# Gather indices held in SBUF for the whole run and edge features loaded two blocks at a time, in a graph layer on one core

## The reference

```
h     = relu(layernorm(x))                       # 12500 x 64
h0    = edge_attr @ W0 + b0
g     = gelu(gelu(h0) @ W1 + b1) @ W2 + b2
score = (h0 + g) @ W3 + b3                       # one row of 64 per edge
msg   = h[src] * score                           # a gathered row per edge
wV    = segment_sum(msg, dst) / max(count(dst), 1)
out   = x + wV @ Wo + bo
```

## Time and profile before

| | |
|---|---|
| device time, median of 3 runs | 4045.06 us (4044.77 to 4045.06) |
| span of the profiled execution | 4042.3 us |
| outside the span, against the median | 2.8 us |
| busy: PE, PEld, DVE, ACT, POOL | 81%, 53%, 27%, 14%, 75% |
| mean granted TensorE clock | 0.785 of full |
| data moved | 174.70 MB, 43 GB/s |

### The profile page before, as it was taken

The page is one execution under the profiler, slowest core; times in us unless marked ns, Lnnn a source line. Parts: engine busy times, 40 slices in busy tenths (PEclk is TensorE's granted clock), DMA queues, the critical chain, the costliest instruction groups (busy, mean ns, idle before and its releaser), DMA issues.

```text
span 4042.3 us, 34777 instructions
## 1 busy us (share of the span) xinstructions
PE 3264.8 (81%) x12308; PEld 2146.4 (53%) x12309; DVE 1084.3 (27%) x2563; ACT 585.2 (14%) x838; POOL 3045.3 (75%) x3228
## 2 busy tenths in 40 slices
PE   4988888888888878888888788888887788888879
PEld 2655555555555555555555555555555555555557
DVE  7322222222222222222222222222222222222234
ACT  4211111111111111111111111111111111111111
POOL 7777777777777777777777777777777777777776
PEclk8977777777777777777777777777777777777778
DMA  5211111111111111111111111111111111111112
GB/s 145 48 40 40 40 40 40 40 40 40 40 40 42 40 40 40 40 40 40 40 40 40 40 40 40 40 40 40 41 41 41 40 40 40 40 40 40 40 37 60
DMA packets 217372, 174.70 MB, mean 43 GB/s; under 512 B 112108, under 2 KB 163821, under 8 KB 216920
## 3 DMA queue, kind: packets, MB, share of 16 engines
q0 software_dynamic: 103136, 105.82, 12.1%
q1 hardware_dynamic: 113536, 64.91, 6.0%
q10 hardware_dynamic: 616, 3.20, 0.2%
HBM read 167.28 MB, written 6.40 MB: 43 GB/s over the span
## 4 chain that ended last, share of the span: by engine, by line
POOL 73%; issue 24%; PE 2%; DVE 0%; DMA 0%; POOLq 0%; ACT 0%; DVEq 0%
POOL rows L332 73%; PE ps_h1a L539 0%; PE ps_h1b L539 0%; PE ps_h0a L463 0%; POOLq L353 0%; PE ps_h1b L471 0%; PE ps_h1a L471 0%; PE ps_sb L482 0%; PE ps_sb L477 0%; PE ps_wa L497 0%; PE ps_h0b L463 0%; DMA rows<-h_rows,idx 0%; PE ps_sb L486 0%; PE ps_sa L482 0%; PE ps_sa L477 0%
## 5 line engine op out<-in xcount | busy, mean ns | idle before, releaser
L332 POOL DMA_INDIRECT rows<-h_rows,idx x3175 | 2999.5, 945 | 967.6 <-issue 966.9
L497 PE MATMUL ps_wa<-ln_sq,msg 128*128 128x128 f32 x1616 | 350.1, 385 | 665.6 <-DVE msg L690 665.5
L497 PEld LDWEIGHTS ps_wa<-ln_sq,msg 128*128 128x128 f32 x1616 | 299.2, 276 | 741.2 <-issue 728.1
L690 DVE TENSOR_TENSOR msg<-ps_sa,rows 128x512 f32<-128x512 f32 x202 | 139.7, 691 | 1403.3 <-DMA rows<-h_rows,idx 1391.0
L690 DVE TENSOR_TENSOR msg<-ps_sb,rows 128x512 f32<-128x512 f32 x201 | 139.0, 692 | 1396.8 <-DMA rows<-h_rows,idx 1382.0
L396 ACT ACTIVATE g<-ps_h1a,wp 128x512 f32<-128x512 f32 x202 | 139.0, 688 | 2383.5 <-PE ps_h1a L471 2383.5
L482 PE MATMUL ps_sa<-w_attr,attr 128*128 128x256 f32 x808 | 405.0, 654 | 0.0
L482 PEld LDWEIGHTS ps_sa<-w_attr,attr 128*128 128x128 f32 x808 | 229.8, 314 | 327.0 <-issue 292.6
L477 PE MATMUL ps_sa<-b_last,wp 1*128 1x512 f32 x404 | 403.1, 1097 | 0.0
L486 PEld LDWEIGHTS ps_sa<-w_gelu,g 128*128 128x128 f32 x1616 | 377.5, 321 | 34.3
L486 PE MATMUL ps_sa<-w_gelu,g 128*128 128x128 f32 x1616 | 367.7, 405 | 0.0
(11 more groups left out here) (94 smaller groups left out, 2381.4 us busy)
## 6 DMA issues: line engine op xcount, KB each, us to landing
attr<-in_edges SPq DMA_DIRECT2D x402, 128.0 KB, 3.0
rows<-h_rows,idx POOLq DMA_INDIRECT x3175, 2.4
xs<-in_x SPq DMA_DIRECT2D x4, 700.0 KB
h_rows<-ln_d ACTq DMA_DIRECT2D x4, 700.0 KB
dst_i<-in_dst SPq DMA_DIRECT2D x1, 1612.0 KB, 27.2
idx<-in_src SPq DMA_DIRECT2D x50, 32.0 KB, 2.3
rows<-in_dst_rows SPq DMA_DIRECT2D x4, 384.0 KB
out<-ln_d SPq DMA_DIRECT2D x1, 1530.0 KB
```

Of the source, the lines that this page charges most:

```text
L332: pool.indirect_dma_start(rows[:, slot, t, :], None, table, bass.IndirectOffsetOnAxis(ap=idx[:, part, at, t:t + 1], axis=0),).then_inc(gat ...
L497: pe.matmul(window[0:m * D, 0:m * WIN], msg[:, s % 2, t:t + m, :].rearrange("p t d -> p (t d)"), hot[:, k, t:t + m, :].rearrange("p t n -> ...
L690: dve.tensor_tensor(msg[:, s % 2, 0:n, :], ps_s[s % 2][:, 0:n * D].rearrange("p (t d) -> p t d", d=D), rows[:, s % G_RING, 0:n, :], ALU.mu ...
```

## The change

1. `idx` has room for all 403 blocks. The first 32 blocks' indices come as before, in four loads. The other 371 blocks' indices are loaded in 3 transfers with runs of 4 KB, a block on each partition, into `src_rows` (which lies in `ln_d`), after `raw_ready` reaches 3. DVE turns them into float32 (`number_src`, in its step 2). In PE's steps 4 to 9 (`turning_step`) `turn` transposes them by 4 matmuls a step with a unit matrix (`diag`), into the bank `ps_h0` of that step, and DVE copies them back as integers to `idx` (`keep_turned`, in its steps 3 to 8). PE waits for that copy ahead of `first(b + 2)`.
2. POOL builds a 128x128 ramp for `diag` at its start, and `gather` waits for indices 4 + 3 times in the run instead of 51 times. SP no longer waits for `msg_done` nor loads groups.
3. `load_attr` brings two blocks by one transfer, in runs of 2 KB, block by block: the even block on partitions 0 to 63, the odd one on 64 to 127. `first` becomes one matmul with 64 rows and 512 columns; the attribute part of `last` becomes 4 matmuls with 64 rows and 128 columns each. The amount of data is the same.

The diff, without the constants, the semaphores' declarations and the branch for wide windows that this input doesn't take:

```diff
@@ -234,27 +246,40 @@
         def tiles_of(b):
             return LAST_TILES if isinstance(b, int) and b == NB - 1 else TILES
+        src_rows = ln_d[:, :, :, :].rearrange("p k n d -> p k (n d)")[:, 0:TURN_CHUNKS, 0:BLOCK]
+        def chunk(c):
+            first = IDX_FIRST + c * P
+            return first, min(P, NB - first)
         block = ctx.enter_context(nc.Block())
         @block.sync
         def _(sp):
-            def load_idx(group, part, n=IDX_GROUP):
-                sp.dma_start(idx[:, part, 0:n, :],
-                             src[bass.ds(group * IDX_GROUP, n), :, :].rearrange("b p t -> p b t")
-                             ).then_inc(idx_in[part], 16)
+            def load_idx(q):
+                at = q * IDX_GROUP
+                sp.dma_start(idx[:, at:at + IDX_GROUP, :],
+                             src[at:at + IDX_GROUP, :, :].rearrange("b p t -> p b t")
+                             ).then_inc(idx_in[q], 16)
+            def load_src(c):
+                first, n = chunk(c)
+                sp.dma_start(src_rows[0:n, c, :].bitcast(I32),
+                             src[first:first + n, :, :].rearrange("b p t -> b (p t)")
+                             ).then_inc(src_in, 16)
             def load_attr(b):
                 n, half = min(2, NB - b), b // 2 % (IN_RING // 2)
-                halves = edges[b:b + n, :, :, :].rearrange("o g f (j c) -> j (g f) o c", j=2)
-                for j in range(2):
-                    sp.dma_start(attr[j * 2 * DE:(j + 1) * 2 * DE, half * 2:half * 2 + n, :, :
-                                      ].rearrange("p o k e -> p o (k e)"), halves[j]
-                                 ).then_inc(attr_in[half], 16)
-            load_idx(0, 0)
+                sp.dma_start(attr[0:n * 2 * DE, half, :],
+                             edges[b:b + n, :, :, :].rearrange("o g f c -> (o g f) c")
+                             ).then_inc(attr_in[half], 16)
+            load_idx(0)
             for c in range(LN_STEPS):
                 cols = slice(c * LN_ROWS, (c + 1) * LN_ROWS)
                 for p0, p1 in ((0, SPLIT), (SPLIT, NP)):
@@ -267,12 +292,12 @@
                                  ).then_inc(rows_in[c], 16)
             sp.dma_start(wp[:, :], weights).then_inc(weights_in, 16)
             load_attr(0)
-            load_idx(1, 1)
+            load_idx(1)
             sp.dma_start(dst_i[:, :, :], dst).then_inc(dst_in, 16)
             for b in range(2, IN_RING, 2):
                 load_attr(b)
-            for part in range(2, IDX_GROUPS):
-                load_idx(part, part)
+            for q in range(2, IDX_GROUPS):
+                load_idx(q)
             sp.dma_start(x_late[:, :, :], x[N_EARLY:N, :].rearrange("(t p) d -> p t d", p=NP)
                          ).then_inc(x_late_in, 16)
@@ -284,27 +309,13 @@
                          ).then_inc(base_in, 16)
             sp.dma_start(top[:, :], bounds_dram[1:2, 0:NB]).then_inc(base_in, 16)
-            def ahead(b, s):
-                if b % 2 == 1 and b + IN_RING - 1 < NB:
-                    sp.wait_ge(score_done, b + 1)
-                    load_attr(b + IN_RING - 1)
-            GROUPS = -(-NB // IDX_GROUP)
-            def group_ahead(group, part, n=IDX_GROUP):
-                for u in range(IDX_GROUP):
-                    ahead(group * IDX_GROUP + u, group * IDX_GROUP + u)
-                sp.wait_ge(msg_done, group * IDX_GROUP + IDX_GROUP)
-                load_idx(group + IDX_GROUPS, part, n)
-            for group in range(GROUPS - IDX_GROUPS):
-                group_ahead(group, group % IDX_GROUPS,
-                            min(IDX_GROUP, NB - (group + IDX_GROUPS) * IDX_GROUP))
-            for b in range((GROUPS - IDX_GROUPS) * IDX_GROUP, NB - IN_RING + 1):
-                ahead(b, b)
+            sp.wait_ge(raw_ready, len(jobs) - LN_STEPS)
+            for c in range(TURN_CHUNKS):
+                load_src(c)
+            for b in range(1, NB - IN_RING + 1, 2):
+                sp.wait_ge(score_done, b + 1)
+                load_attr(b + IN_RING - 1)
             for half in range(2):
                 k0, k1 = half * len(groups) // 2, (half + 1) * len(groups) // 2
@@ -322,16 +333,20 @@
         def _(pool):
             pool.iota(iota_i[:, :], pattern=[[1, WIN]], base=0, channel_multiplier=0
                       ).then_inc(set_up, 1)
+            pool.iota(diag_i[:, :], pattern=[[1, P]], base=0, channel_multiplier=-1
+                      ).then_inc(diag_set, 1)
             def gather(b, s, table):
-                slot, part, at = s % G_RING, s // IDX_GROUP % IDX_GROUPS, s % IDX_GROUP
-                if at == 0:
-                    pool.wait_ge(idx_in[part], uses(b, IDX_GROUP * IDX_GROUPS) * 16)
+                slot = s % G_RING
+                if s < IDX_FIRST and s % IDX_GROUP == 0:
+                    pool.wait_ge(idx_in[s // IDX_GROUP], 16)
+                if s >= IDX_FIRST and (s - IDX_FIRST) % P == 0:
+                    pool.wait_ge(idx_ready, ((s - IDX_FIRST) // P + 1) * (TILES // TURN_TILES))
                 for t in range(tiles_of(b)):
                     pool.indirect_dma_start(
                         rows[:, slot, t, :], None, table,
-                        bass.IndirectOffsetOnAxis(ap=idx[:, part, at, t:t + 1], axis=0),
+                        bass.IndirectOffsetOnAxis(ap=idx[:, s, t:t + 1], axis=0),
                     ).then_inc(gathered[slot], 16)
             for b in range(RAW):
@@ -458,12 +473,11 @@
             def first(b, s):
                 if s % 2 == 0:
-                    pe.wait_ge(attr_in[s // 2 % (IN_RING // 2)], uses(b, IN_RING) * 32)
-                for j in range(2):
-                    mm = pe.matmul(ps_h0[s % 2][:, j * 2 * P:(j + 1) * 2 * P], w_in[:, j, :],
-                                   attr[:, s % IN_RING, :, :].rearrange("p k e -> p (k e)"),
-                                   start=(j == 0), stop=(j == 1), skip_group_check=True)
-                mm.then_inc(h0_done, 1)
+                    pe.wait_ge(attr_in[s // 2 % (IN_RING // 2)], uses(b, IN_RING) * 16)
+                o = s % 2
+                pe.matmul(ps_h0[s % 2][:, :], w_in[o * 2 * DE:(o + 1) * 2 * DE, o, :],
+                          attr[o * 2 * DE:(o + 1) * 2 * DE, s // 2 % (IN_RING // 2), :], start=True, stop=True
+                          ).then_inc(h0_done, 1)
             def second(b, s):
@@ -477,10 +491,12 @@
                 pe.matmul(ps_s[s % 2][:, :], one_row.to_broadcast([1, P]),
                           b_last[0:1, :, :].rearrange("p t d -> p (t d)"), start=True, stop=False,
                           skip_group_check=True)
-                for k in range(2):
-                    four = ps_s[s % 2][:, :].rearrange("p (j k c) -> p k j c", j=2, k=2)[:, k, :, :]
-                    pe.matmul(four, attr[:, s % IN_RING, k, :],
-                              w_attr[:, :].rearrange("p (j c) -> p j c", j=2), start=False, stop=False, skip_group_check=True)
+                o = s % 2
+                for j in range(TILES // 2):
+                    pe.matmul(ps_s[s % 2][:, j * 2 * D:(j + 1) * 2 * D],
+                              attr[o * 2 * DE:(o + 1) * 2 * DE, s // 2 % (IN_RING // 2), j * P:(j + 1) * P],
+                              w_attr[o * 2 * DE:(o + 1) * 2 * DE, o * 2 * D:(o + 1) * 2 * D],
+                              start=False, stop=False, skip_group_check=True)
                 pe.wait_ge(g2_done, b + 1)
                 for j in range(TILES // 2):
                     mm = pe.matmul(ps_s[s % 2][:, j * 2 * D:(j + 1) * 2 * D],
@@ -550,6 +566,28 @@
                                    start=(t == 0), stop=(t == LATE_TILES - 1), skip_group_check=True)
                 mm.then_inc(proj_done, 1)
+            def turn(k, s):
+                c, half = k // 2, k % 2
+                n = chunk(c)[1]
+                pe.wait_ge(src_ready, c + 1)
+                pe.wait_ge(diag_ready, 1)
+                for j in range(TURN_TILES):
+                    t = half * TURN_TILES + j
+                    mm = pe.matmul(ps_h0[s % 2][:, j * P:j * P + n], src_rows[0:n, c, t:BLOCK:TILES],
+                                   diag[0:n, 0:n], start=(j == 0), stop=(j == TURN_TILES - 1),
+                                   skip_group_check=True)
+                mm.then_inc(turned, 1)
+            def turning_step(k, b, summed):
+                second(b, b)
+                turn(k, b)
+                summed(b - 3, b - 3)
+                last(b - 1, b - 1)
+                pe.wait_ge(idx_ready, k + 1)
+                first(b + 2, b + 2)
             def steps(first_block, end, summed):
@@ -592,7 +630,9 @@
             with pe.If(flag < WIN):
                 narrow(0, 0)
                 last(2, 2)
-                steps(4, EARLY_BLOCKS + 3, narrow)
+                for k in range(TURNS):
+                    turning_step(k, 4 + k, narrow)
+                steps(4 + TURNS, EARLY_BLOCKS + 3, narrow)
                 pe.wait_ge(g2_done, EARLY_BLOCKS + 3)
```

(32 more changed lines are left out.)

16 lines of the change are left out of this document (14 added, 2 removed).

## The result

| | before | after |
|---|---|---|
| device time, median of 8 runs | 4044.98 us (4044.48 to 4045.24) | 4054.60 us (4050.83 to 4060.08) |
| span of the profiled execution | 4042.3 us | 4052.8 us |
| PE busy, mean granted clock | 81%, 0.785 | 88%, 0.762 |

The ratio is 1.0025, with a 95% interval from 1.0016 to 1.0034: slower by 9.6 us. The interval leaves out no change. The prediction took 0.2% as the least that a measurement tells from no change; the median lies above that, and the interval takes it in. The median lies in the stated range (4044 to 4056), 3.8 us above the predicted 4050.8. The predicted growth was 0.14%, the measured one 0.25%. After's profiled execution took 4054.6 us, 1.8 more than its span. The 2.8 us that the prediction put outside the span of before mixed two executions, and that is most of why the spans differ by 10.5 us and the medians by 9.6.

What follows compares the result with a forecast made beforehand. POOL's closed chain of gathers was taken to set the time, with PE's own chain close behind at the end. Terms 0 + 0 + 1.3 + 4.4 = +5.7 us took 4045.06 to 4050.8 us; range 4044 to 4056.

Steps and rivals of the forecast that it cites:

- POOL's pace and start: POOL's gathers: second ramp, removed index waits and the indices' new place in SBUF each cost or gain 0.
- The conversions' hold: DVE's three conversions in number_src hold up POOL's gathers: 1.3 us taken, between 0 and 3.6.
- The turning steps: PE's and DVE's turning of indices stays off POOL's path: 27 of 40 us of cover used, cost 0.
- The changes of form: PE's catch-up: three row-count changes a step at 0.2 us, +0.59 us a step, +4.4 us at the end.
- Rival A: Form changes cost nothing or PE's slack is larger, so POOL alone sets the end: 4046.4 us; chance 0.23.
- The slack: PE's reserve in the catch-up before added step time moves the end: 0.3 us subtracted in the sum.
- Rival B: PE's clock falls in the catch-up, losing 3.1 us in a single step: 4053.9 us; chance 0.09.
- signs of being wrong: POOL waits for PE or DVE; steps keep 5.93; clock leaves 0.99; last gather over 3 us from 4030.5.
- My reason against: Against rival B: L477 with 1 row takes 18% of PE's step now and the clock stays.
- the half clock's price for every change: Upper end for PE's form changes: 24 changes x 0.3 - 0.3 = 6.9 us.
- The middle is covered: Mid-run, PE idles 3 of 20 us, so +1.2 to 1.8 us in 20 costs nothing.
- The chance of 0.83: Chance given to the same time, within 0.2% (8.1 us); faster had 0.03, slower 0.14.

Runs made afterwards that it cites:

- idx_only: The change with load_attr, first, last and the shape of attr as before it; 4046.12 us, against 4045.51 for the kernel before.
- rows_128: The change with first and the attribute part of last over all 128 rows, zero weights for the other block; 4045.84 us, before 4045.51.
- tail_128: The change with first (from block 396) and the attribute part of last (from block 393) over 128 rows; 4045.15 us, before 4044.56.
- attr_only: The kernel before with load_attr, first, last and the shape of attr from the change; 4054.85 us, against 4045.51 for before.
- after_bias_128: The change with the 1-row bias matmul run over 128 rows, the parts with 64 rows kept; 4051.57 us, before 4044.64.
- all_128: rows_128 with the 1-row bias matmul over 128 rows too; 4044.94 us, against 4044.64 for the kernel before.

## Why the prediction was right, and where it fell short

**POOL's pace and start: right.** Waits removed 0, indices in another place 0, start 0 (the first gather at 3.34 us, behind the second ramp, which ends at 1.2).

**The conversions' hold: mis-sized.** The term was 1.3 us between 0 and 3.6. In after the three conversions take 1.89 us together, 0.63 each and not 1.22, and lengthen one gather by 0.16 and one by 0.05:

```profile
94.81 1.10 POOL L347 DMA_INDIRECT rows<-h_rows,idx  x1 [0.30 <-issue]
95.10 1.89 DVE L813 CAST ln_d<-ln_d 128x1024 f32<-128x1024 int32 x3
96.21 1.00 POOL L347 DMA_INDIRECT rows<-h_rows,idx  x1 [0.30 <-issue]
```

The same three conversions added 0.07 to 0.55 us in the other kernels that have them, the most in idx_only (0.48 and 0.08), so the size differs from one execution to the next. The halved length that I expected is there. The full block for the length of the operation, which the Trainium skill states (SBUF — State Buffer, "Who interferes with whom") and which I put at 1.2 us by my estimate, isn't what the rows show. The last gather starts 0.4 us late, and the conversions are half of that.

**The turning steps: right.** Message 2 came 7.0 us late (96.92 against 89.94) where 16 were allowed; message 1 was already 5.1 us late (89.14 against 84.00), while the clock was still low, so the index transfers, issued at 73.7 us, held up nothing. The steps took 8.3 us each, and POOL waited for none of it.

**The changes of form: right in place and size.** Predicted 0.2 us a change and steps of 6.5, measured 0.195 and 6.54; 24 changes in the catch-up are 4.7 us, as the term had it. The single distances were a little off: from `first` to the next part 1.06 us, where 1.1 to 1.25 was expected. The Trainium skill (TensorEngine Tiling (Array Packing), "Key Properties") says that a change of tiling mode drains the engine. The step times of every kernel with parts on 64 rows agree with a price for it, 0.195 us here. Rival A (no cost, 0.23) is out: rows_128 against after. The slack was 0.15 us and not 0.3 to 0.4: the 0.39 that I read was the wait of PE's load, and PE's own sums sit between the last score and the last sums.

**The clock: the step that failed.** The sum took the catch-up "in the catch-up it isn't: 7 steps x 0.59 + 3 x 0.19", at the full clock from its first steps, as in before, and had no term for a late rise. That term measured 5.35 us, more than the 4.7 of the changes. Rival B, put at 0.09, came nearest, with 4053.9 against 4054.6: it let the half-used parts cost the full clock, 3.1 us for one step. But it had the clock fall from its full level; the runs showed it staying low from the start of the catch-up, for two steps, on top of the forecast's own term. One of my signs of being wrong was met: the granted clock from 3976 to 4012 us left 0.99 and was 0.82. What spoke for it was in the earlier trace rows: the catch-up begins at 0.50, right behind the projection, so the question was not whether the clock falls but how soon it rises, and a half-empty `first` stands second in that very step. I argued from a clock that stays up. My reason against, that the 1-row bias matmul doesn't keep the clock down, was no reason: that part was in both kernels.

**The range** held, in part by luck. Its upper end, 4055.6, was made of a full hold by the conversions (3.6) and of the half clock's price for every change (6.9). Neither came in full: they measured 0.2 and 4.7. The late rise, which had no term, filled the room made for them. "The middle is covered" was right for its own reason: tail_128. The chance of 0.83 for "within 0.2%" was too high, since the forecast's sum of 5.7 was only 2.4 us from the bound.

Open stays why `first` and not the attribute part delays the rise, with 512 columns on 64 rows each, and why it didn't at the start of attr_only. Open is also what makes executions like the 4060.08 and the 4050.83 of after. A long one was caught in a profile, the 4061.58 of after_bias_128. There the gathers took 0.947 us at the median, and the last one starts at 4037.3, 7.7 us later than in after: most of the 10 us between this execution and its kernel's median. That the others have the same cause wasn't seen.

## What to carry to other kernels

Ask of the bounding engine's chain where it ends, and what runs behind or beside its last link: an engine with 19% idle over the run had next to none in the last 60 us before the end of the sums, and there alone the change was paid for. Don't cut matmuls down to half the rows when zeros in the weights do the same with all rows: the columns cost the same, and each change of form cost 0.2 us here. After a phase at the half clock, look at what the first parts of the next phase are made of.

## What was not expected of the hardware

- With PE busy without a gap, the granted clock stayed at 0.50 for 11.7 to 15.2 us where the catch-up began with `first` on 64 rows, and for 3.6 to 6.2 us where all or most of it had 128. At the start of the run one kernel of five with such a `first` didn't show it.
- With the 1-row matmul over 128 rows too (all_128), the clock's mean from 200 to 3900 us was 0.84, against 0.78 in before, and PE was busy 2757 us instead of 3003: more rows, fewer busy microseconds, and the same end.

```profile
200.00:3900.00 3700.00, 2757.17 (x11876) 1771.97 (x11875) 911.86 (x2223) 509.81 (x743) 2796.70 (x2965) 0.84 0.18 40
```

- A gather was held off through eight DVE operations in a row, and was only slowed by one conversion.
